# Mixture of experts and gated recurrence on one core: down products nearer to their unit, sums, scatters and gathers re-placed, all side work laid anew

## The reference

```python
# layer 0, tokens xf [8192, 256]
shared = silu(xf @ w1) * (xf @ w3) @ w2                      # 256 -> 512 -> 256
s = sigmoid(concat([xf, tf], -1) @ router_W)                 # tf: a vector for each sequence
idx = top_k(s + router_bias, 2); gates = s[idx] / sum(s[idx])
h = gelu(xf @ W1e[e]); y = h @ W2e[e]                        # 8 experts, 256 -> 256 -> 256
x = x + (shared + sum_e gate_e * y_e) / 3
# layer 1, over the 256 tokens of each sequence, h starts as cond
gate = sigmoid(h @ Wh.T + z_t @ Wz.T + b)
h = tanh(h * (1 - alpha) + gate * z_t)                       # z_t: token t of x
x = x + all h
```

## Time and profile before

| | |
|---|---|
| median of three runs | 770.74 us |
| the profiled execution | 774.02 us |
| its span (first to last instruction) | 772.1 us |
| TensorE busy | 711.0 us |
| VectorE, ScalarE, GpSimd busy | 549.0, 472.3, 270.6 us |
| mean granted clock of TensorE | 0.967 |
| DMA | 124.83 MB, mean 162 GB/s |

### The profile page before, as it was taken

One profiled execution on the slowest core, in us unless ns is written; L12 is line 12 of the kernel. 1 busy time (PEld: TensorE's weight loads), 2 busy tenths in 40 slices (PEclk: granted clock), 3 DMA queues, 4 the chain that ended last, 5 costly groups with the idle time before them and its releaser, 6 DMA issues.

```text
span 772.1 us, 23818 instructions
## 1 busy us (share of the span) xinstructions
PE 711.0 (92%) x8562; PEld 512.1 (66%) x8562; DVE 549.0 (71%) x2014; ACT 472.3 (61%) x1347; POOL 270.6 (35%) x284
## 2 busy tenths in 40 slices
PE   5899898998999999999989999999999999999763
PEld 3454486645788756898568896565888555686442
DVE  4787651458777698876678886897975678866754
ACT  4746464634567755677666677556876645676433
POOL 2037455166542156452075025772040173003100
PEclk9999999999999999999999999999999999999865
DMA  8836799774996675895859454357484354123101
GB/s 279 323 110 226 222 235 281 199 193 117 205 233 167 172 174 141 203 213 164 205 144 253 99 146 165 118 166 132 101 203 135 111 164 118 43 90 121 39 14 42
DMA packets 166466, 124.83 MB, mean 162 GB/s; under 512 B 118706, under 2 KB 147156, under 8 KB 166356
## 3 DMA queue, kind: packets, MB, share of 16 engines
q1 hardware_dynamic: 150436, 79.19, 42.1%
q0 software_dynamic: 14368, 41.96, 17.7%
q10 hardware_dynamic: 1552, 2.15, 0.8%
HBM read 39.90 MB, written 55.84 MB: 124 GB/s over the span
## 4 chain that ended last, share of the span: by engine, by line
PE 68%; DVE 12%; ACT 7%; DMA 6%; issue 4%; SPq 1%; POOL 1%; ACTq 0%; DVEq 0%; POOLq 0%
PE bank L1731 64%; PE bank L1930 2%; DMA xe<-x_slots_even 2%; PE bank L1865 1%; DVE full L1492 1%; DVE pre L1553 1%; DVE hid_low L1499 1%; DVE taken L1550 1%; SPq L956 1%; DMA xe<-x_slots_odd 1%; ACT th L1249 1%; ACT hs_high L1257 1%; DMA x_res<-in_x_dram 1%; POOL y_got L1129 1%; DVE r_sum L1518 1%
## 5 line engine op out<-in xcount | busy, mean ns | idle before, releaser
L1731 PE MATMUL bank<-xe,w1e_high 128*128 128x128 f16 x1360 | 216.6, 220 | 8.1 <-DMA xe<-x_slots_even 3.6
L1731 PE MATMUL bank<-xs,w_high 128*128 128x512 f16 x512 | 168.9, 385 | 5.0 <-DVE w_low L1669 2.8
L1731 PE MATMUL bank<-xe,w1e_low 128*128 128x128 f16 x680 | 146.9, 219 | 0.0
L1499 DVE TENSOR_TENSOR hid_low<-full,hid_high 128x512 f16<-128x512 f32 (+1 forms) x152 | 103.2, 679 | 45.1 <-ACT hid_high L1202 34.9
L1731 PEld LDWEIGHTS bank<-xe,w1e_high 128*128 x1360 | 114.3, 97 | 26.5 <-issue 14.0
L1249 ACT ACTIVATE th<-bank 128x64 f32<-128x64 f32 x256 | 56.9, 222 | 101.4 <-PE bank L1731 97.3
L1550 DVE SCALAR_TENSOR_TENSOR taken<-th,zq 128x64 f32<-128x64 f32 x256 | 58.2, 227 | 78.0 <-ACT th L1249 73.6
L1257 ACT ACTIVATE hs_high<-pre 128x64 f16<-128x64 f32 x256 | 65.5, 256 | 73.7 <-DVE pre L1553 62.5
L1731 PEld LDWEIGHTS bank<-hs_high,gwt_high 128*128 128x128 f16 x1024 | 70.1, 97 | 51.9 <-ACT hs_high L1257 37.5
L1070 POOL TENSOR_TENSOR fence_pool<-zero 128x1 f32<-128x1 f32 x12 | 2.8, 234 | 278.2 <-DMA y_slots_odd<-y_pair 84.7
L1731 PE MATMUL bank<-hs_high,gwt_high 128*128 128x32 f16 x1024 | 79.0, 178 | 22.5 <-ACT hs_high L1257 21.9
(11 more groups left out here) (156 smaller groups left out, 1705.8 us busy)
## 6 DMA issues: line engine op xcount, KB each, us to landing
y_slots_even<-y_pair SPq DMA_DIRECT2D x45, 256.0 KB
y_slots_odd<-y_pair SPq DMA_DIRECT2D x37, 256.0 KB
x_res<-in_x_dram SPq DMA_DIRECT2D x16, 512.0 KB
out_dram<-o_tok SPq DMA_DIRECT2D x32, 256.0 KB, 3.1
x_tok<-in_x_dram SPq DMA_DIRECT2D x14, 512.0 KB, 5.0
x_slots_even<-zeros POOLq DMA_DIRECT2D x1, 4096.0 KB, 18.1
x_slots_odd<-zeros POOLq DMA_DIRECT2D x1, 4096.0 KB, 15.2
y_got<-in_L_cond_W1e_dram SPq DMA_DIRECT2D x4, 512.0 KB, 12.9
```

The costliest lines, as they stand in the source:

```text
L1499: dve.tensor_tensor(hid[1][:, u.i % NR, some], full32[:, u.i % 2, some], hid[0][:, u.i % NR, some], ALU.subtract).then_inc(s_lo, 1)
L1731: return pe.matmul(out_ap, w, mov, start=start, stop=stop, skip_group_check=True)
```

## The change

The diff has five kinds of edits, and no instruction is added or taken away: each engine has the same number of each kind.

1. **Down products.** For ten shared units (`SOON`) the down product moves one unit ahead (i + 1), so that units with two of them arise. `act_residual` follows the last one.
2. **Sums.** `FINISH`, `SUM_AT` and `AT_ONCE` shift for groups 12, 14 and 15; group 12 has both halves in unit 133 (`LATE`). Group 15's four tiles were all summed in unit 151, now two in 151 and two in 152.
3. **Routing.** Logits of section 2 at unit 33 (34 before), ranks of section 1 at unit 13 (12 before).
4. **DMAs.** The scatters of sections 0 and 1 start some units earlier, those of section 2 go without step pace for longer, those of sections 3 to 5 wait for steps 3 to 9 earlier; the gathers of sections 3 and 4 wait for no step at all. Five stores of the output stand one to two units later.
5. **All tables of the recurrence** (`PE_AT`, `ACT_AT`, `DVE_AT`) are new; of some 700 lines two are shown.

```diff
-FINISH = [FIRST_SHARED[_q] + GROUP for _q in range(N_GROUPS)]
-for _q, _u in enumerate((37, 40, 43, 61, 64, 67, 83, 86, 89, 104, 107, 111, 132, 135, 138, 151)):
-    FINISH[_q] = _u
-AT_ONCE = (15,)
-SUM_AT = {_q: [FINISH[_q] + 2 - (_q in AT_ONCE), FINISH[_q] + 3 - (_q in AT_ONCE)] for _q in range(N_GROUPS) if AHEAD[_q]}
+FINISH = [37, 40, 43, 61, 64, 67, 83, 86, 89, 104, 107, 111, 131, 135, 141, 151]
+AT_ONCE = ()
+SUM_AT = [[39, 40], [42, 43], [45, 46], [63, 64], [66, 67], [69, 70], [85, 86], [88, 89], [91, 92], [106, 107], [109, 110], [113, 114], [133, 133], [137, 138], [143, 145], [152, 153]]
+SOON = (9, 82, 128, 129, 131, 132, 133, 134, 135, 138)
...
-LOGITS_UNIT = [2, 9, 34, 56, 90, 111]
-RANKS_AFTER = [2, 3, 3, 4, 4, 4]
+LOGITS_UNIT = [2, 9, 33, 56, 90, 111]
+RANKS_AFTER = [2, 4, 3, 4, 4, 4]
...
-SCATTER_AT = [[_f + _j * _a // _b for _j in range(_n)] for _n, _f, _a, _b in zip(
-    SECTIONS, (7, 18, 39, 63, 96, 118), (1, 1, 1, 1, 2, 1), (2, 1, 1, 1, 3, 1))]
-GATHER_AT = [[_f + _j * _a // _b for _j in range(_n)] for _n, _f, _a, _b in zip(
-    SECTIONS, (34, 58, 80, 100, 128, 148), (1, 1, 1, 1, 1, 1), (2, 2, 2, 2, 2, 2))]
+SCATTER_AT = [
+    [3, 3, 4, 4, 5, 5, 6, 6, 7, 7, 8, 8], [16, 17, 18, 19, 20, 21, 22, 23, 24, 25, 26, 27],
...
+GATHER_AT = [
+    [34, 34, 35, 35, 36, 36, 37, 37, 38, 38, 39, 39], [57, 57, 58, 58, 59, 59, 60, 60, 61, 61, 62, 62],
...
 SCATTER_STEP = {
-    2: (-1, -1, -1, 0, 1, 2, 3, 4, 5, 6, 7, 8, 9, 10, 11, 12, 13, 14, 15, 16, 17, 18, 19, 20),
...
+    2: (-1, -1, -1, -1, -1, -1, -1, -1, -1, -1, 0, 1, 2, 3, 4, 5, 6, 7, 8, 9, 10, 11, 12, 13),
...
-    3: (123, 124, 125, 125, 129, 130, 131, 131, 133, 134, 135, 135, 139, 140, 140, 141, 143, 144, 144, 145, 146, 146, 147, 148),
-    4: (187, 187, 188, 188, 189, 189, -1, -1, 191, -1, -1, -1, -1, -1, -1, -1, -1, -1, -1, -1, -1, -1, -1, 192),
+    3: (-1, -1, -1, -1, -1, -1, -1, -1, -1, -1, -1, -1, -1, -1, -1, -1, -1, -1, -1, -1, -1, -1, -1, -1),
+    4: (-1, -1, -1, -1, -1, -1, -1, -1, -1, -1, -1, -1, -1, -1, -1, -1, -1, -1, -1, -1, -1, -1, -1, -1),
...
 PE_AT = {
...
+    (132, 25): ((HIGH, 190),), (133, 1): ((STEP, 190),), (133, 8): ((HIGH, 191),), (133, 9): ((STEP, 191),),
+    (134, 11): ((FILL, 48), (FILL, 49), (HIGH, 192), (STEP, 192),), (134, 16): ((HIGH, 193),),
...
+        def down_at(i):
+
+            return i + DOWN_LAG - (i in SOON)
...
                 for q in range(N_GROUPS):
-                    if u.i == (FIRST_SHARED[q] + MID + DOWN_LAG if AHEAD[q] else max(FIRST_SHARED[q] + MID, FINISH[q]) + 2):
+                    if u.i == (down_at(FIRST_SHARED[q] + MID - 1) + 1 if AHEAD[q] else max(FIRST_SHARED[q] + MID, FINISH[q]) + 2):
                         act_residual(q, gap)
...
-                pair_down, shared_down = units_at(u.i - DOWN_LAG, EXPERT), units_at(u.i - DOWN_LAG, SHARED)
-                if shared_down and u.kind != SHARED:
-                    down_shared(shared_down, gap)
+                pair_down = units_at(u.i - DOWN_LAG, EXPERT)
+                shared_downs = [units_at(i, SHARED) for i in range(u.i - DOWN_LAG, u.i)
+                                if units_at(i, SHARED) and down_at(i) == u.i]
+                if shared_downs and u.kind != SHARED:
+                    down_shared(shared_downs[0], gap)
```

More of the change, by code:

```diff
@@ new lines @@
+    (66, 13): ((HIGH, 46),), (66, 14): ((STEP, 46), (FILL, 12), (HIGH, 47), (FILL, 13), (STEP, 47),),
+    (67, 5): ((HIGH, 48),), (67, 6): ((STEP, 48),), (67, 13): ((HIGH, 49), (STEP, 49),),
+    (68, 6): ((HIGH, 50), (STEP, 50),), (68, 13): ((HIGH, 51),), (69, 2): ((STEP, 51),),
+    (69, 13): ((HIGH, 52), (STEP, 52), (FILL, 14),), (69, 14): ((FILL, 15), (HIGH, 53), (STEP, 53),),
+    (70, 6): ((HIGH, 54), (STEP, 54),), (70, 12): ((HIGH, 55),), (70, 13): ((STEP, 55),),
+    (71, 6): ((HIGH, 56), (STEP, 56),),
@@ new lines @@
+    (112, 6): ((FILL, 38), (FILL, 39), (HIGH, 152),), (112, 7): ((STEP, 152),), (112, 19): ((HIGH, 153),),
+    (112, 20): ((STEP, 153),), (113, 12): ((HIGH, 154),), (113, 15): ((FILL, 40), (FILL, 41),),
+    (113, 19): ((STEP, 154),), (114, 9): ((HIGH, 155), (STEP, 155),), (115, 3): ((HIGH, 156),),
+    (115, 4): ((STEP, 156),), (115, 10): ((HIGH, 157),), (115, 11): ((STEP, 157),),
+    (116, 12): ((HIGH, 158), (STEP, 158),), (117, 4): ((HIGH, 159),), (117, 5): ((STEP, 159),),
+    (117, 12): ((HIGH, 160),), (118, 2): ((STEP, 160),), (118, 11): ((HIGH, 161),),
@@ new lines @@
+    (148, 6): ((STEP, 224),), (148, 15): ((HIGH, 225),), (148, 16): ((STEP, 225),),
+    (148, 27): ((HIGH, 226), (STEP, 226),), (148, 35): ((HIGH, 227),), (149, 0): ((STEP, 227),),
+    (149, 10): ((HIGH, 228),), (149, 11): ((STEP, 228),), (150, 7): ((HIGH, 229), (STEP, 229),),
+    (150, 16): ((HIGH, 230), (STEP, 230),),
+    (151, 6): ((HIGH, 231), (STEP, 231), (FILL, 58), (FILL, 59), (HIGH, 232), (STEP, 232),),
+    (151, 14): ((HIGH, 233), (STEP, 233),), (151, 15): ((HIGH, 234),), (152, 0): ((STEP, 234),),
@@ new lines @@
+    (154, 7): ((STATE, 242), (GATE, 243),),
+    (154, 10): ((STATE, 243), (GATE, 244), (STATE, 244), (GATE, 245), (STATE, 245), (GATE, 246), (STATE, 246),),
+    (155, 3): ((GATE, 247), (STATE, 247), (GATE, 248),), (155, 4): ((STATE, 248), (GATE, 249), (STATE, 249),),
+    (155, 8): ((GATE, 250),), (156, 9): ((STATE, 250),), (157, 8): ((GATE, 251),),
+    (158, 0): ((STATE, 251), (GATE, 252), (STATE, 252),), (158, 1): ((GATE, 253),), (158, 8): ((STATE, 253),),
+    (159, 3): ((GATE, 254), (STATE, 254), (GATE, 255), (STATE, 255),),
@@ L473 @@
+    (155, 4): ((MIX, 244), (REST, 244), (MIX, 245),), (156, 0): ((REST, 245), (MIX, 246), (REST, 246),),
+    (156, 5): ((MIX, 247), (REST, 247), (MIX, 248),), (157, 4): ((REST, 248), (MIX, 249),), (157, 6): ((REST, 249),),
+    (158, 2): ((MIX, 250),), (158, 4): ((REST, 250), (MIX, 251),),
+    (158, 5): ((REST, 251), (MIX, 252), (REST, 252), (MIX, 253), (REST, 253), (MIX, 254), (REST, 254), (MIX, 255),),
+    (160, 4): ((REST, 255),),
 }
@@ L479 @@
                   + [(LOGITS_UNIT[_n] + RANKS_AFTER[_n], (RANKS, _n)) for _n in range(NS)]
-                  + [(_u, (SUM, (_q, _kc))) for _q in SUM_AT for _kc, _u in enumerate(SUM_AT[_q])]):
+                  + [(_u, (SUM, (_q, _kc))) for _q, _at in enumerate(SUM_AT) for _kc, _u in enumerate(_at)
+                     if _kc == 0 or _u > _at[0]]):
     assert _u not in MISC, (_u, _item)
     MISC[_u] = _item
-SPARE = [MISC[_u] for _u in sorted(MISC)]
+LATE = {_at[0]: (SUM, (_q, 1)) for _q, _at in enumerate(SUM_AT) if _at[1] == _at[0]}
+SPARE = [_at[_u] for _u in sorted(MISC) for _at in (MISC, LATE) if _u in _at]
+assert all(UNITS[_u].kind == SHARED == UNITS[_u + 1].kind for _u in SOON)
 TAKEN = 3.0e38
@@ L1629, in body @@
                     for kc in range(KC):
-                        if AHEAD[q] and u.i == SUM_AT[q][kc]:
+                        if AHEAD[q] and u.i == SUM_AT[q][kc] and (kc == 0 or u.i not in LATE):
                             add_part(q, kc)
@@ L1635, in body @@
                     product(u)
+                if u.i in LATE:
+                    gap()
+                    add_part(*LATE[u.i][1])
                 first_section(u, 1, gap)
@@ L1966, in body @@
                 if u.kind == SHARED:
-                    if shared_down:
-                        down_shared(shared_down, gap)
+                    for v in shared_downs:
+                        if v is not shared_downs[0]:
+                            gap()
+                        down_shared(v, gap)
                     gap()
+                if u.i in LATE:
+                    misc(*LATE[u.i], gap)
                 for q in range(N_GROUPS):
```

690 lines of the change are left out of this document (333 added, 357 removed), and 14 rows, old and new, of tables (GATHER_AT, OUT_AT, SCATTER_AT, SCATTER_STEP).

## The result

The changed kernel takes 775.38 us (median of 20 runs, 771.67 to 784.66), the kernel before, beside it, 770.92 us (20 runs, 765.26 to 774.2). The ratio is 1.0062 (95% interval 1.004 to 1.0084): slower by 0.6%, where 765.9 us and faster had been forecast, and just outside the range of 760 to 775. The run of 784.66 us lies over 1.5% above the fastest, counts as slow and is left out of the ratio.

The account below looks back on a forecast made before the run. TensorE, busy 711.0 of 772.1 us, was taken as the bound, with some 20 us to win at most. Terms -0.65 - 0.85 + 0.6 - 2.5 - 1.4 = -4.8 from 770.7 gave 765.9 us; range 760 to 775.

Parts of the forecast that it names:

- the term for section 0's scatters and the clear: First transposed pairs near 92 us: TensorE's wait goes with earlier scatters, clear behind them; -0.85 us, bounds -0.85 to +4.
- slower rival: Moved down products: VectorE's low parts come late, TensorE waits 0.85 us in each of ten units; 774.4 us, chance 0.18.
- Ranks of section 1: Ranks product at 75 us, one unit later: TensorE's wait for VectorE's mask goes; -0.65 us, bounds 0 to -0.65.
- Earlier scatters: Section 0's scatters sooner, first transposes ending some 4 us earlier: TensorE's wait at 92.24 goes, -0.85 us.
- Logits: Section 2's logits in unit 33: transpose wait grows 2.59, low-part wait of 2.67 mostly goes; +0.6 us, bounds -0.1 to +2.6.
- The recurrence's waits: TensorE's waits for `hs_high` or `hs_low`, 92 to 720 us: new tables shrink 6.7 us by 2.5, bounds 0 and -5.
- The tail: From the last shared unit to step 240: four gated rows moved behind VectorE's product; -1.4 us, bounds 0 and 3.4.

Follow-up runs that it names:

- experiment 1: Changed kernel with the clear of the odd slots back between section 0's twelfth and thirteenth scatters: 764.77 us, ratio 0.9912 to the kernel before.
- experiment 2: Kernel before with section 0's scatters at units 3 to 8, so the clear comes behind all 24: 779.97 us, ratio 1.012 to the kernel before.
- experiment 8: Changed kernel, clear in the middle, group 15's last two tiles again summed ahead of VectorE's last shared product: 768.84 us, ratio 0.9936 to the kernel before.

## Why the prediction was wrong

**The step that failed** is the term for section 0's scatters and the clear: it took -0.85 us, with an upper bound of +4. It measured +11.6 us (experiment 1). With one number changed the loss goes, and with one number changed the kernel before has it (9.3 us, experiment 2). Of it 8.2 us are there at unit 16; where the rest of it lies the profiles don't show.

The mechanism was named, the clear beside the first transposes, and so was the page's rule that would make it dear. The price was wrong, in two ways. The 4.02 and 4.57 us of the earlier trace rows are what SyncE's queue took to issue the transposes, and not how long these took to land. The chain of the kernel before has that for the first pair:

```profile
88.27 3.67 DMA xe<-x_slots_even
```

So the pair took 3.67 us with no clear beside it, and not 1.34. And the 4.57 us are from a stretch where the neighbours were of another kind: from 200 to 212 us GpSimd's queue moved 0.66 MB and SyncE's own 2.06, while a clear is 4 MB in packets of 4 KB, and took 89.5% of the engines' time. The bound from above should have been the clear's 15.2 us, nearly all of which came: the first pair landed when the clear did, after 13.83 us. It was also held that only the third pair could be late; the first one was. No rival had this; the slower one named late low parts.

**That slower rival** did not happen. The ten down products brought no such waits: TensorE waits for `hid_low` 0.7 us in the whole run.

**Ranks of section 1**: -0.65 forecast, about -1.3 by unit 15, but worth nothing at unit 16, where TensorE waits for the pair.

**Earlier scatters**, apart from the clear: -0.85 forecast, nothing measured.

**Logits**: +0.6 forecast; from unit 33 to 40 the first run is 0.5 us longer than before (36.6 to 36.1), which is within what like kernels differ by. The growth of one wait by 2.6 us to 4.3 and the end of the other came as worked out.

**The recurrence's waits**: -2.5 forecast from 6.7 us. They did not shrink. The view of waits of the run with the clear moved, from 90 to 712 us:

```profile
PE bank L1751 <- ACT hs_high L1274: 4.7, 9, 1.1
...
PE bank L1751 <- DVE hs_low L1576: 2.2, 2, 2.1
```

That is 6.9 us. The forecast's 6.7 left out a wait of 0.2; by the same view over the same stretch the kernel before has 6.9 as well (3.9 for `hs_high`, 3.0 for `hs_low`). Step 192 does follow sooner, 7.1 us behind step 191 where the forecast had 8, in ScalarE's timeline of the changed kernel:

```profile
639.10 0.22 ACT L1266 ACTIVATE th<-bank 128x64 f32<-128x64 f32 x1
...
646.18 0.23 ACT L1266 ACTIVATE th<-bank 128x64 f32<-128x64 f32 x1 [1.85 <-PE bank L1751]
```

but the slack it brings wasn't what those waits needed: in the run with the clear moved only 1.1 of the 6.9 us lie behind 560 us (1.5 before).

**The tail**: -1.4 forecast, -3.1 in the changed kernel (728.54 to 744.98 for the same stretch as above, 16.4 us) and -3.3 with the clear moved, near the upper bound given. The order of VectorE's rows was worth 2.0 of it. The rest, 1.3, goes with the half clock in the one profile from which the forecast was made, and is no gain of the change (experiment 8).

```profile
728.54 0.60 ACT L1235 ACTIVATE full<-bank 128x512 f32<-128x512 f32 x1
...
744.98 0.22 ACT L1266 ACTIVATE th<-bank 128x64 f32<-128x64 f32 x1 [2.09 <-PE bank L1751]
```

Without the failed step the sum was near: 765.9 forecast, 764.8 measured with the clear in the middle. That is in part luck. The waits that were to give 2.5 us gave nothing, and a tail that gave 2.0 in place of 1.4, and a stretch from unit 40 to 50 from which nothing had been forecast, made up for it.

## What to carry to other kernels

When a table moves DMAs, look not only at the ones it names but at what stood between them: here twelve scatters went ahead of a 4 MB clear, and the clear came to lie beside the one transfer that TensorE waited for. Where a small transfer comes to lie beside a large one with larger packets (here 256 bytes against 4 KB), take the large one's whole time as the upper bound, and not what a small one cost beside other small ones. Read such a price from the time to landing, not from how long the queue took to issue. A bulk write without a deadline belongs where nothing that an engine waits for is moved beside it: at the start it delayed a load of tokens by 4.3 us, later it delayed later pairs, and only among the first twelve scatters or just behind them did it cost nothing that could be measured. A gain or loss of a microsecond or two that stands in a single profile can be chance; look at the same stretch in every other kernel that has the same instructions there.

## What the runs showed of the hardware

Two queues shared the DMA engines by packets and not by bytes: 1040 packets of 4 KB against 1387 of 256 bytes in 13 us, and so 12 to 1 in bytes. The transposes of small packets beside a bulk write finished when the bulk write did: in 13.83 us beside 4 MB, in 8.18 beside 2 MB, in 3.76 with none.

TensorE's granted clock at one place, with the same instructions and equal waits ahead of it (0.86 and 1.18 us), differed between two profiles: the last shared down product ran at 0.63 us a matmul in that of the kernel before, and at 0.38 in that of the second experiment.

The earlier start in the table made section 0's scatters little earlier: the last one was issued at 82.25 us instead of 85.85, four units sooner by the table, since GpSimd's issuing of 24 of them (0.97 to 1.8 us each, 0.30 between) was the limit. Of these 3.6 us, 1.5 are the place of the clear's own issue, which now stood behind; with the clear back in the middle the last scatter was issued at 84.39.
